# Layer 0 of a graph network on one core: run maxima by two chained scans, the score factor moved into the query weights, position counts taken by an accumulator

## The reference, cut to what matters

```python
Q = (x @ Wq).reshape(n, H, DH); K = (x @ Wk).reshape(n, H, DH); V = (x @ Wv).reshape(n, H, DH)
q_dst = Q[dst] + rel_q[edge_type].reshape(-1, H, DH)
k_src = K[src] + rel_k[edge_type].reshape(-1, H, DH) + (time_emb @ Wt + bt).reshape(-1, H, DH)
euclid = jnp.sum(q_dst * k_src, axis=-1) / np.float32(np.sqrt(DH))
euclid = euclid * decay
hyp = -hyp_beta[None, :] * man_dist * decay
alpha = jax.nn.sigmoid(logit_alpha)[None, :]
logits = alpha * euclid + (1.0 - alpha) * hyp
seg_max = jax.ops.segment_max(logits, dst, num_segments=n)
ex = jnp.exp(logits - seg_max[dst])
denom = jax.ops.segment_sum(ex, dst, num_segments=n)
agg = jax.ops.segment_sum(v_src * (ex / denom[dst])[..., None], dst, num_segments=n)
```

## Time and profile before

| | us |
|---|---|
| median of 3 runs | 4200.18 (4199.8 to 4203.0) |
| the profiled execution's own time | 4200.05 |
| its span | 4198.2 |
| DVE busy over the span | 3360.9 (80%) |
| PE busy | 3262.7 (78%) |
| POOL busy | 2059.0 (49%) |
| ACT busy | 1979.8 (47%) |

### The profile page before, as it was taken

One profiled execution on the slowest core, in us unless ns is written; L12 is line 12 of the kernel. 1 busy time (PEld: TensorE's weight loads), 2 busy tenths in 40 slices (PEclk: granted clock), 3 DMA queues, 4 the chain that ended last, 5 costly groups with the idle time before them and its releaser, 6 DMA issues.

```text
span 4198.2 us, 85753 instructions
## 1 busy us (share of the span) xinstructions
PE 3262.7 (78%) x31253; PEld 2706.8 (64%) x31253; DVE 3360.9 (80%) x7173; ACT 1979.8 (47%) x5714; POOL 2059.0 (49%) x2454
## 2 busy tenths in 40 slices
PE   1388898899999632688747788686999999689995
PEld 1155555566666321677636778654999999689995
DVE  5599999999999644999768878767666666789997
ACT  2355555556666222899735666611222222234443
POOL 0356677777777410588612100000555555368883
PEclk7699999999999766788868899888999999899998
DMA  4756666667677301000012111132444444223331
GB/s 91 227 164 177 175 181 186 186 197 203 201 204 203 83 14 41 9 14 14 12 58 83 58 43 47 49 135 92 123 130 125 126 124 125 70 85 124 129 129 62
DMA packets 290761, 471.98 MB, mean 112 GB/s; under 512 B 79648, under 2 KB 218850, under 8 KB 290194
## 3 DMA queue, kind: packets, MB, share of 16 engines
q1 hardware_dynamic: 236178, 302.04, 23.7%
q0 software_dynamic: 54144, 164.25, 14.0%
HBM read 407.19 MB, written 58.93 MB: 111 GB/s over the span
## 4 chain that ended last, share of the span: by engine, by line
DVE 40%; PE 34%; issue 10%; POOL 6%; ACT 5%; DMA 3%; SPq 2%; DVEq 0%; POOLq 0%; ACTq 0%
POOL arena_a L1232 6%; PE psum L3838 5%; PE psum L3854 4%; PE psum L3789 4%; PE psum L3787 4%; PE psum L3754 2%; DVE arena_a L1975 2%; DVE arena_c L2025 2%; DVE arena_a L1971 2%; PE psum L3813 2%; PE psum L3426 2%; DVE arena_a L3334 2%; PE psum L3836 2%; PE psum L3785 2%; DVE msg_parts L3576 1%
## 5 line engine op out<-in xcount | busy, mean ns | idle before, releaser
L1232 POOL DMA_INDIRECT arena_a<-src_table,src_tix x808 | 841.2, 1041 | 347.9 <-issue 226.1
L3558 POOL TENSOR_SCALAR node_hot<-arena_c 128x128 fp32r<-128x128 f32 x575 | 367.0, 649 | 902.7 <-DVE arena_c L3446 567.8
L3576 DVE SCALAR_TENSOR_TENSOR msg_parts<-psum,msg_parts 128x512 fp32r<-128x512 f32 (+2 forms) x644 | 425.6, 661 | 260.2 <-ACT msg_parts L3725 227.3
L3276 POOL TENSOR_SCALAR node_hot_dst<-arena_c 128x128 fp32r<-128x128 f32 x587 | 382.5, 668 | 123.7 <-DVE arena_c L3680 67.9
L3725 ACT ACTIVATE msg_parts<-psum 128x512 fp32r<-128x512 f32 (+2 forms) x325 | 186.5, 574 | 520.3 <-PE psum L3789 520.3
L3787 PE MATMUL psum<-arena_c,arena_a 128*128 128x128 bf16 x3675 | 406.4, 220 | 0.0
L3789 PE MATMUL psum<-arena_c,arena_a 128*128 128x128 bf16 x3675 | 406.4, 220 | 0.0
L1423 ACT ACTIVATE arena_a<-arena_a 128x128 f32<-128x128 f32 x808 | 239.6, 297 | 280.0 <-DVE arena_a L1973 277.3
L3785 PE MATMUL psum<-src_tix,arena_a 128*128 128x128 bf16 x1225 | 272.4, 222 | 70.9 <-DVE arena_a L3462 37.2
L3154 PE MATMUL psum<-arena_a,arena_c 128*128 128x150 f32 x1800 | 293.2, 330 | 41.9 <-ACT arena_c L3096 41.8
L2538 PE MATMUL psum<-weights,ident 128*128 128x512 f32 x606 | 286.9, 609 | 40.0 <-DVE arena_a L1971 40.0
(11 more groups left out here) (645 smaller groups left out, 9511.5 us busy)
## 6 DMA issues: line engine op xcount, KB each, us to landing
arena_a<-bucket_rows SPq DMA_DIRECT2D x150, 384.0 KB
arena_b<-near_keys SPq DMA_DIRECT2D x101, 252.0 KB
arena_a<-bucket_rows SPq DMA_DIRECT2D x50, 448.0 KB
arena_a<-bucket_lists SPq DMA_DIRECT2D x25, 896.0 KB
pair_counts<-arena_c SPq DMA_DIRECT2D x25, 800.0 KB
arena_a<-bucket_lists SPq DMA_DIRECT2D x25, 704.0 KB
arena_a<-src_table,src_tix POOLq DMA_INDIRECT x808
arena_c<-edge_attr SPq DMA_DIRECT2D x101, 128.0 KB
```

What stands on the lines that cost most here:

```text
L1232: e.indirect_dma_start(out_, None, table, bass.IndirectOffsetOnAxis(ap=idx, axis=0)).then_inc(sem, 16)
L3276: return e.tensor_scalar(node_hot3[at % RING_H][:, i, :], iota_row, dst_lo[:, b, t:t + 1], None, ALU.is_equal)
L3558: return e.tensor_scalar(node_hot[at % RING_M][:, i, :], iota_row, src_lo[:, b, 2 * k + j:2 * k + j + 1], None, ALU.is_equal)
L3576: e.scalar_tensor_tensor(out=to[:, 1, 0:nt, :], in0=bank[at % 4][:, 0:nt * P].rearrange("p (t f) -> p t f", f=P), scalar=0.0, in1=to[:, 0, ...
```

## The change

Four edits, all in layer 0.

1. **Maxima.** The forward scan now writes one row, and the backward scan takes that row, not the logits, as its input. A run's last edge then holds the run's maximum and the backward scan carries it to all of the run. The maximum operation is gone. The second scan waits for the first.
2. **Score factor.** `hrow[:, 1, :]` is multiplied once, in the prologue, into the query columns of `Wqkv` and the query rows of `relb`; the multiplication in each step is gone. PE's first product waits for this (`lists_set` at 8) and no more for `d_weights`.
3. **Counts.** In place of a comparison and a sum there is one `scalar_tensor_tensor` with `accum_out`, which compares, multiplies by ones, and accumulates.
4. **The other branch** (`dve_l0_any`), taken when some destinations lie too far apart, gets the same edits and its own message function. It does not run with these inputs: the trace holds none of its lines.

```diff
+            own.mark(e.tensor_tensor(relb[:, :, D:2 * D], relb[:, :, D:2 * D], bc(btb[:, :], 1, NET), ALU.add))
+            for q_ in (relb[:, 0, 0:D], relb[:, 1, 0:D]):
+                own.mark(e.tensor_tensor(by_head(q_), by_head(q_), bc(hrow[:, 1, :], 2, DH), ALU.mult))
+            own.settle()
+            e.tensor_tensor(by_head(Wqkv[:, 0:D]), by_head(Wqkv[:, 0:D]), bc(hrow[:, 1, :], 2, DH), ALU.mult).then_inc(g.lists_set, 1)
...
-                own.step(e.tensor_scalar(first_p, last_row, node_id[:, b:b + 1], None, ALU.is_le))
-                own.step(e.tensor_reduce(te[:, b:b + 1], first_p, AX, ALU.add))
+                own.step(e.scalar_tensor_tensor(out=first_p, in0=last_row, scalar=node_id[:, b:b + 1], in1=bc(ones[:, 0], 1, TT),
+                                                op0=ALU.is_le, op1=ALU.mult, accum_out=te[:, b:b + 1]))
...
-                own.step(e.tensor_scalar(keys_b, keys_b, node_id[:, b:b + 1], None, ALU.is_le))
-                e.tensor_reduce(cnt[:, b:b + 1], keys_b, AX, ALU.add).then_inc(g.pos_counted, 1)
+                e.scalar_tensor_tensor(out=keys_b, in0=keys_b, scalar=node_id[:, b:b + 1], in1=ones[:, :],
+                                       op0=ALU.is_le, op1=ALU.mult, accum_out=cnt[:, b:b + 1]).then_inc(g.pos_counted, 1)
...
-                    e.tensor_tensor_scan(tl[:, 1, :], runs[s2][:, 0, :], tl[:, 0, :], -BIG, ALU.add, ALU.max)
-                    e.tensor_tensor_scan(tl[:, 2, ::-1], runs[s2][:, 1, ::-1], tl[:, 0, ::-1], -BIG, ALU.add, ALU.max).then_inc(g.scanned, 1)
+                    own.step(e.tensor_tensor_scan(tl[:, 2, :], runs[s2][:, 0, :], tl[:, 0, :], -BIG, ALU.add, ALU.max))
+                    e.tensor_tensor_scan(tl[:, 1, ::-1], runs[s2][:, 1, ::-1], tl[:, 2, ::-1], -BIG, ALU.add, ALU.max).then_inc(g.scanned, 1)
                     e.wait_ge(g.scanned, i2 + 1)
-                    own.step(e.tensor_tensor(tl[:, 1, :], tl[:, 1, :], tl[:, 2, :], ALU.max))
                     e.tensor_tensor(tl[:, 0, :], tl[:, 0, :], tl[:, 1, :], ALU.subtract).then_inc(g.less_ready, 1)
...
                     own.mark(e.tensor_tensor(other, other, d2, ALU.mult))
-                    own.mark(e.tensor_tensor(v3(eu), v3(eu), bc(hrow[:, 1, :], 1, TPB), ALU.mult))
                     own.settle()
...
-            e.wait_ge(g.d_weights, 464)
+            e.wait_ge(g.lists_set, 8)
```

More of the change, by code:

```diff
@@ L1699, in dve_turn_weight @@
             e.tensor_copy(dst_, bank[6][0:width, 0:parts]).then_inc(g.trw_dve, 1)
+        by_head = lambda v: v.rearrange("p (h w) -> p h w", h=H)
         def dve_prologue(e, own):
@@ L1807, in dve_prologue @@
             own.step(e.tensor_tensor(hrow[:, 2, :], hrow[:, 2, :], hrow[:, 3, :], ALU.mult))
-            own.step(e.tensor_tensor(relb[:, :, D:2 * D], relb[:, :, D:2 * D], bc(btb[:, :], 1, NET), ALU.add))
+            own.mark(e.tensor_tensor(relb[:, :, D:2 * D], relb[:, :, D:2 * D], bc(btb[:, :], 1, NET), ALU.add))
[3 more added lines that the diff above has]
+            e.tensor_tensor(by_head(Wqkv[:, 0:D]), by_head(Wqkv[:, 0:D]), bc(hrow[:, 1, :], 2, DH), ALU.mult).then_inc(g.lists_set, 1)
             e.wait_ge(g.d_lists, 304)
@@ L1928, in dve_l0_messages, with dve_any_messages @@
                             bc(msg_w[s][:, :, D:D + H], 3, DH), ALU.mult).then_inc(g.gs_used, 1)
+        def dve_any_messages(e, k):
+            s, r = k % 2, k % RING
+            e.wait_ge(g.exp_ready, k + 1)
+            if k >= 2:
+                e.wait_ge(g.sums_pe, 4 * (k - 1))
+            e.tensor_tensor(msg[s][:, :, 0:D].rearrange("p t (h w) -> p t h w", h=H),
+                            GS[r][:, :, D:2 * D].rearrange("p t (h w) -> p t h w", h=H),
+                            bc(msg[s][:, :, D:D + H], 3, DH), ALU.mult).then_inc(g.gs_used, 1)
         def dve_run_rows(e, k):
@@ L2099, in dve_l0_any @@
                         dve_same_half(e, i3, hf, dst_col, 0)
-                    dve_l0_messages(e, i3)
+                    dve_any_messages(e, i3)
                 if b1:
@@ L2103, in dve_l0_any @@
                     own.step(e.tensor_tensor(v3(t1), bc(d2, 2, H), bc(hrow[:, 2, :], 1, TPB), ALU.mult))
-                    own.step(e.tensor_tensor(v3(eu), v3(eu), bc(hrow[:, 1, :], 1, TPB), ALU.mult))
                     own.step(e.tensor_tensor(eu, eu, t1, ALU.subtract))
```

## The result

| | before | changed |
|---|---|---|
| median, us | 4200.14 (4199.8 to 4203.0, 4 runs) | 4141.2 (4137.2 to 4143.36, 4 runs) |
| ratio, 95% interval | | 0.9861 (0.9849 to 0.9873) |
| the profiled execution's own time | 4200.05 | 4143.36 |

The change gives 58.9 us. The faster side was right, the size was not.

What follows compares the result with a forecast made beforehand. DVE was taken to bound layer 0's stretches A and C, POOL's gathers B. Savings of 25.0 in A, 18.5 in C, 0.5 in last steps and 1.0 at the seam, 45.0 in all, gave 4155 us from 4200.05; range 4142 to 4177.

Steps and rivals of the forecast that it cites:

- The faster side: Whole kernel: faster than before by more than 0.2% (8 us), given 95%.
- B itself. I leave it as it is.: Key-gather stretch of layer 0: no gain, as POOL sets the pace; 10 us either way kept for the range.
- B: Layer 0's loop, blocks 27 to 51, with key gathers; POOL sets the pace, forecast gain nothing.
- A with the seam: Layer 0's loop, blocks 2 to 26 (L1854 runs), 25.0 us, plus 1.0 at the passage to the key gathers.
- C: Layer 0's loop, blocks 52 to 101, DVE without a gap: 50 x 0.37 = 18.5 us gain.
- B gets faster: Rival in the key-gather stretch: collisions of POOL and DVE fall apart by 0.6 us a step, 4141 us; 5%.
- the prologue is free: Score factor's three added multiplications before the loop, hidden in DVE's 30.54 us of idleness: priced at nothing, 1 us without cover.
- the dip: Where key gathers begin, PE stood 1.85 us and L2573 took 1.41 us longer; forecast to go, gaining 1.0 us.
- the bound in C: Rival in blocks 52 to 101: PE becomes the bound, 4164 us at half the gain kept, 4173 at all; 12%.
- The seam's 1.0 us: Passage from L1854's steps to the key gathers: PE's slow L2573 no longer delays DVE, gain 1.0 us.
- Half rate of the accumulating instruction: Rival in blocks 2 to 26: the new count runs at half rate, 1.91 us instead of 1.70, 4176 us; 9%.
- Slower: Rival in the key-gather stretch: PE's clock falls to 1.2 GHz; 4263 us over half of it; 3%.

Runs made afterwards that it cites:

- e3_counts: The kernel before with the edit of the counts alone, in blocks 2 to 51: 4182.73 us, ratio 0.9956.
- e1_scans: The kernel before with the edit of the maxima alone (two chained scans, no maximum operation): 4185.21 us, ratio 0.9961.
- e2_factor: The kernel before with the edit of the score factor alone: 4185.55 us, ratio 0.9961.
- e4_pair_keys: The changed kernel with comparison and sum back for the keys alone: 4150.75 us, ratio 0.9882 to the kernel before.

## Why the prediction was wrong

**The step that failed** is "B itself. I leave it as it is." B gave 12.5 us. Between the two profiled executions, against which the sum was made, the forecast was short by 11.7: A with the seam gave 2.5 less, C and what stands behind it 1.7 more, B 12.5 more. The median lies another 2.2 us below its profiled execution, where that of before lies on it. The mechanism was in the text (gathers stretch beside DVE's long instructions with two SBUF inputs), and so, nearly, was the size, 10 us either way; what was missing was the rule by which the row's 0.94 to 1.87 us come about. "Nothing says which way they shift" was not so: the trace of before held it. Each stretched gather in B there ends 0.82 us after such an instruction, or 0.76 after the second scan, and two of the edits shorten the way to one: from the keys' landing to L1926 by the count (643.07 - 642.41 = 0.66 us before, 662.05 - 661.63 = 0.42 after), from L1926's end to L1935's by the maxima (0.26). That the maxima's edit takes 0.26 off L1935's stretch in one kind of step and 0.19 off the scans' in the other could have been worked out from the trace of before; that the count's comes off L1926's shows where that edit is in and nowhere else: 0.30 us a step in `e3_counts` and 0.32 in the changed kernel, 0.50 to 0.55 in the kernel before and in `e1_scans`, `e2_factor` and `e4_pair_keys` (over the last 16 steps of B).

The rival "B gets faster" had this case at 14.4 us and 5%, with the time 4141. It is what happened, and it was left at 5% because the text had no rule for which way the collisions would shift.

**Right.** The sides and sizes elsewhere: A with its seam 23.5 (26.0 forecast), C 20.7 (19.0). The accumulating instruction takes 1.052 us and its read-out 0.08, mostly inside; the messages follow 1.10 us after L1860's start (472.62 to 473.72), 1.07 forecast, and a step of A is 0.99 shorter (1.00 forecast). L1823 begins at 110.82 us, with 29.31 us of idleness still ahead of it: the prologue is free. L2585 at the seam waits 1.05 and takes 2.23 us: the dip is gone (what that was worth stands below). PE didn't become the bound in C. The clock stayed at full in B on the first chip.

**Mis-sized terms.** The seam's 1.0 us isn't found: the slow L2573 begins at 522.70 us, behind the first key gather at 521.62, where POOL goes on with 0.30 us between gathers whatever DVE waits for. A's 23.5 are 23.8 from 24 steps, 0.5 between the last count and the first key gather, and 0.8 lost by a later start (211.3 against 210.5). The maxima give 0.20 a step, not 0.23: both scans take 0.42 where I took 0.39 for the second. Another 0.06 a step came unforeseen: the logits (L2043 before, L2056 after) took 0.29 us in nearly each step of before and take 0.22 or 0.23 now, because a gather no longer starts with them. Together a step of C gives 0.41 where 0.37 was forecast. The waits for the keys came to 19.3 us, not 25 or more, as the gathers themselves are faster.

**Half rate of the accumulating instruction** has fallen. Over 808 columns 1.052 us is the 1.00 us of the row without an accumulator and 0.05 more. The Trainium skill (Vector Engine (DVE) Microarchitecture Reference, section Points that are easy to get wrong) says that this form with two non-bf16 SBUF sources halves throughput; by that rule it would be an estimated 1.84 us here, as the prediction worked it out, and the measurement decides against it. The Trainium skill (SBUF — State Buffer, section Who interferes with whom) says that a DVE instruction with two SBUF inputs contends with a GpSimd instruction that reads SBUF and that a sum never does. The trace agrees for the long instructions and the sums, and not for one short instruction (below).

**Slower** had 3%, for a clock that falls in B. On the first chip nothing of it is seen. On the two others the clock falls, though in A as well as in B, with the change and without it, and the change loses 0.3 to 0.8%. My chance of 95% for "faster" held for the chip on which before and changed were timed; as a statement on any chip it was too high, and no row of the one trace I had could say so.

## What to carry to other kernels

Where GpSimd issues gathers back to back and VectorE seems to wait for it, the pace can still be partly VectorE's: list the gathers longer than the usual, subtract the end of the long two-input instruction beside each, and if the difference is one constant, the distance between such instructions can be priced. Here the price of two memsets came out at 0.48 us a step where 0.49 was due by the distance measured; the distance expected beforehand was 0.38. Price the whole ring of gathers, not one hold, since a gather that gets free earlier meets the next instruction at another point. And an edit that makes TensorE stop at another place of a step should be tried on more than one chip.

## What the runs showed of the hardware

- In the traces of eight kernels on the first chip, of the gathers of layer 0's loop that began while one DVE instruction of over 0.3 us ran, the middle eight in ten ended 0.81 to 0.83 us after its end beside three instructions with two SBUF inputs (419 in L1932, 747 in L1950, 772 in L1996, or their counterparts), and took an unchanged 0.94 to 0.95 us inside a sum (784 in L2039) or an instruction with one of its inputs in PSUM (1527 in L1986, L1988 and L1990). The 1.03 of many key gathers is L1996's hold.
- It isn't so for every instruction with two SBUF inputs: beside the key count over 128 columns (L1867, 0.35 us), the 22 gathers that began up to 0.10 us behind its start took 0.94 or 0.95 us, and only the three that began 0.10 to 0.13 behind it ended 0.82 after its end. Beside the second scan of before (L2016) a held gather ends 0.75 or 0.76 us after its end. Why isn't shown.
- It works the other way too, by a little: L2056 takes 0.29 us instead of 0.22 where a gather starts 0.03 or 0.04 us behind it (96 of 101 steps before), and 0.22 or 0.23 where it starts 0.16 to 0.18 behind.
- The same program took 4200 us on one chip and 4501 to 4533 on two others. On those TensorE's granted clock was 0.84 to 0.91 over A and 0.81 to 0.86 over B in the traces read, where the first chip has 0.99 to 1.00, and there the order of two kernels turned round.
